# Top-384 sorting network of a 16-expert feed-forward layer: the stages that make runs of 256 go from whole-stage order to two interleaved streams

## What is computed

```python
for i in range(E):                                   # E = 16
    gate_feature = hidden_states * pe[i] @ gate_w + gate_b      # 625 x 768
    gate_weight, gate_idx = jax.lax.top_k(gate_feature, K)      # K = 384
    gate_weight = jax.nn.softmax(gate_weight, axis=-1)
    gathered = jnp.take_along_axis(hidden_states, gate_idx, axis=-1)
    y = y + _moe_mlp(gathered * gate_weight, eg_w[i], eu_w[i], ed_w[i])
```

## Time and profile before

| | us |
|---|---|
| median of 3 runs | 6935.59 (6921.98 to 6955.94) |
| the profiled execution | 6922.95, span 6921.2 |
| DVE busy | 5366.8, 78% of the span |
| PE busy | 5904.7, 85% |
| POOL busy | 3589.6, 52% |
| ACT busy | 2729.2, 39% |
| sort of expert 0 begins | 1287.67 |
| a turn of the loop | 334.0 and 335.0, by turns |

### The profile page before, as it was taken

One profiled execution on the slowest core, in us unless ns is written; L12 is line 12 of the kernel. 1 busy time (PEld: TensorE's weight loads), 2 busy tenths in 40 slices (PEclk: granted clock), 3 DMA queues, 4 the chain that ended last, 5 costly groups with the idle time before them and its releaser, 6 DMA issues. The chain is left out here.

```text
span 6921.2 us, 74102 instructions
## 1 busy us (share of the span) xinstructions
PE 5904.7 (85%) x16985; PEld 3098.9 (45%) x16985; DVE 5366.8 (78%) x6633; ACT 2729.2 (39%) x4297; POOL 3589.6 (52%) x3692
## 2 busy tenths in 40 slices
PE   7979988889797878788888888888888888888988
PEld 5545544445444444343434344434343444444554
DVE  3012003599999999999999999999999999998950
ACT  0000000344544545454545454545454545444531
POOL 2324015356565656565656565656565656555640
PEclk9989999999999999999999999999999999999999
DMA  3356247000000000000000000000000000001001
GB/s 90 102 141 170 104 122 188 26 21 14 14 14 15 14 14 14 14 14 14 14 14 14 14 14 14 14 24 4 28 0 28 14 14 14 14 14 48 15 35 50
DMA packets 118060, 260.81 MB, mean 38 GB/s; under 512 B 39164, under 2 KB 49922, under 8 KB 117682
## 3 DMA queue, kind: packets, MB, share of 16 engines
q1 hardware_dynamic: 70322, 180.18, 7.3%
q0 software_dynamic: 47360, 77.17, 5.0%
HBM read 222.43 MB, written 34.58 MB: 37 GB/s over the span
## 5 line engine op out<-in xcount | busy, mean ns | idle before, releaser
L1183 PE MATMUL mask_ps<-key,neg_ident 125*125 125x480 f32 (+7 forms) x4128 | 1917.1, 584 | 566.5 <-DVE key L1557 563.8
L1285 POOL TENSOR_TENSOR pay<-pay_side,pay 125x240 int32<-125x240 int32 (+6 forms) x1104 | 1045.4, 947 | 1163.7 <-DVE pay L1580 1159.5
L1441 ACT COPY mask_ps<-key 125x960 f32<-125x960 f32 (+7 forms) x1136 | 952.5, 838 | 1462.6 <-DVE pay L1597 762.1
L1183 PEld LDWEIGHTS mask_ps<-key,neg_ident 125*125 125x125 f32 x4128 | 744.7, 194 | 1449.5 <-DVE key L1557 952.1
L1580 DVE COPY_PREDICATED pay<-mask_ps,pay 125x480 f32<-125x480 int32 (+5 forms) x1104 | 1233.8, 1118 | 48.1 <-PE mask_ps L1183 39.4
L1277 POOL TENSOR_TENSOR pay_side<-pay 125x240 int32<-125x240 int32 (+6 forms) x1104 | 1041.7, 944 | 407.5 <-DVE pay L1597 263.7
L1547 DVE TENSOR_TENSOR key<-mask_ps,key 125x480 f32<-125x480 f32 (+5 forms) x1104 | 1088.7, 986 | 60.2 <-PE mask_ps L1183 54.2
L1557 DVE TENSOR_TENSOR key<-mask_ps,key 125x480 f32<-125x480 f32 (+5 forms) x1104 | 1092.1, 989 | 8.3
L1454 ACT COPY pay_side<-pay 125x480 f32<-125x480 f32 (+6 forms) x1104 | 612.4, 555 | 451.8 <-POOL pay L1285 233.2
L1183 PE MATMUL mask_ps<-key_top,neg_ident 125*125 125x480 f32 (+3 forms) x1472 | 591.9, 528 | 229.2 <-DVE key_top L1557 216.6
L1597 DVE COPY_PREDICATED pay<-mask_ps,pay_side 125x480 f32<-125x480 int32 (+6 forms) x1104 | 744.1, 674 | 41.8 <-DVE pay L1580 39.9
(11 more groups left out here) (184 smaller groups left out, 6056.0 us busy)
## 6 DMA issues: line engine op xcount, KB each, us to landing
w_rel<-L_gnn_W SPq DMA_DIRECT2D x16, 2304.0 KB, 23.3
w_exp<-L_ffn_ed_w SPq DMA_DIRECT2D x16, 2304.0 KB, 8.3
messages_dram<-y_out SPq DMA_DIRECT2D x16, 1875.0 KB
w_exp<-L_ffn_eg_w SPq DMA_DIRECT2D x16, 1152.0 KB, 5.4
w_exp<-L_ffn_eu_w SPq DMA_DIRECT2D x16, 1152.0 KB, 7.8
root_w<-L_gnn_root SPq DMA_DIRECT2D x2, 2304.0 KB
w_exp<-L_ffn_sg_w SPq DMA_DIRECT2D x4, 1152.0 KB, 5.9
w_exp<-L_ffn_su_w SPq DMA_DIRECT2D x4, 1152.0 KB, 8.7
```

The source lines that it names most:

```text
L1183: last = pe.matmul(mask, neg_ident[0:TP, 0:TP], operand, start=False, stop=True, skip_group_check=True)
L1285: pool.tensor_tensor(second, shares(pay_was(turn, u), turn, u)[1].bitcast(I32), first, ALU.subtract).then_inc(pays_taken, 1)
L1441: act.copy(seed_of(turn, u), compared(turn, u)[0]).then_inc(seeded, 1)
```

## The change

The ranges of units change, and with them the value of `streams`:

- `streams` now covers stages 28 to 35 as well (`LARGE`). Only `JOIN` is left in whole-stage order.
- Stage 29 is two units of 480 columns where it was one of 960; stage 54 is one of 960 where it was two of 480. A regular turn has 93 units as before: 75 woven, 16 of stages 28 to 35, 2 of `JOIN`. `SORTED` is 37 where it was 39, so exponentials, weights and scaling of the expert before come two units earlier in a turn.
- Stage 28's parts take rows 0 to 31 and 64 to 95 of the 128 places, and 32 to 63 and 96 to 127 (two pieces of 480 columns each), and the first part of stage 30 is one of its three groups instead of two. So stages 28 to 30 can follow each other with one unit between.
- Two points, the first units of stages 28 and 31 (`JOINT`), still need every unit before them. There POOL takes the pays of both units before it adds, and ACT and POOL wait for the second pays of the unit before.

```diff
 UNITS = [(s, part, parts) for s, stage in enumerate(STAGES)
-         for parts in [1 if APART <= s < NS - 1 and comparisons(stage) <= MASK else 2] for part in range(parts)]
+         for parts in [1 if s > JOIN and comparisons(stage) <= MASK else 2] for part in range(parts)]
+JOINT = [APART, STAGES.index(("sort", RUN // 2, RUN // 16))]
@@ class Turn
-        self.needs = [max(u - 1, 0) if u < streams else stages.index(s) for u, s in enumerate(stages)]
+        self.joint = [stages.index(s) for s in JOINT if s in stages]
+        self.needs = [max(u - 1, 0) if u < streams and u not in self.joint else stages.index(s)
+                      for u, s in enumerate(stages)]
@@
-OPENING = Turn(HALVES + WHOLES, len(HALVES), 0)
-REGULAR = Turn(WOVEN + WHOLES, len(WOVEN), 1, OPENING)
+LARGE = [unit for unit in WHOLES if unit[0] < JOIN]
+OPENING = Turn(HALVES + WHOLES, len(HALVES + LARGE), 0)
+REGULAR = Turn(WOVEN + WHOLES, len(WOVEN + LARGE), 1, OPENING)
@@ def part_of
-    cut = (view.shape[dim] + 1) // 2
+    cut = 1 if view.shape[dim] == 3 else (view.shape[dim] + 1) // 2
@@ def part_in_banks
+            if s == APART:
+                quarters = view.rearrange("p n (two x) -> p n two x", two=2)
+                half = quarters.shape[3] // 2
+                return quarters[:, :, :, part * half:part * half + half]
@@ sort of the gpsimd block
-                    if u == turn.streams and u > 1 and turn.shared[u - 2]:
+                    apart = u < turn.streams and u not in turn.joint
+                    if not apart and u > 1 and turn.shared[u - 2] and u <= turn.streams:
                         take_pays(turn, i, u - 2)
-                    ahead = u - 2 if u < turn.streams else u - 1
-                    if ahead >= 0 and turn.shared[ahead]:
+                    ahead = u - 2 if apart else u - 1
+                    if ahead >= 0 and turn.shared[ahead] and u - 1 not in turn.joint:
                         take_pays(turn, i, ahead)
```

## The result

The changed kernel takes 6863.51 us (median of 4 runs, 6852.20 to 6873.89), the kernel before 6932.36 in the runs beside it. The ratio is 0.9902, with a 95% interval of 0.9887 to 0.9917: 69 us or 1.0% faster. The forecast was 6806 us, with 6755 to 6881 as its range. So the direction and the range held, but only a little over half of the 129 us came. The profiled execution took 6858.79 us, its span is 6857.0, which is 64.2 us shorter than the span before.

A forecast was written before the change was run, and what follows sets the result against it. DVE was taken as full before stage 28, and stages 28 to 35 as bound by the order of work. -7.9 us a turn, 126 us over 16 turns, 129 with stage 54, gave 6806 us, range 6755 to 6881.

The forecast's parts named there:

- the order's price: DVE, stages 28 to 35: stream order saves 0.40 us on each of 15 units, -6.0 us a turn.
- the waits of both joints: Stages 28 and 31: new DVE waits for masks and POOL's sums add 3.4 us a turn.
- -7.9 us a turn: Sum for a turn's stages 28 to 35: -6.0 - 2.16 + 0.2 - 4.1 + 0.8 + 3.4.
- The share, -2.2 us: Stages 28 to 35: POOL at 4/8 instead of 3/8 takes 1620 columns a turn of second pays from DVE.
- The waits that go: Stages 28 to 35: DVE's waits for masks and POOL vanish in stream order, -4.1 us a turn.
- the 0.8 us a turn kept for what is late next: Allowance for masks before first pays, POOL's sum and its longer difference ahead of `JOIN`: +0.8 us a turn.
- Two units for one, and one for two, about 0: Stage 29 costs 0.2 us a turn more, stage 54 gives 0.2 back; nothing for work moving two units forward.
- joints at their dear end: Stages 28 and 31: two waits of 3.6 us, with the pays 8.1 us a turn; total 6881 us.
- 1: DVE's own waits are free, the 0.40 us has another cause and stays: 6902 us; chance 0.03.
- 2: POOL's additional work holds up DVE, losing 6.8 us of a turn's 7.9: 6915 us; chance 0.04.
- 3: Waits at stages 28 and 31 and before first pays give everything back: within 20 us of 6935; chance 0.03.
- 4: Joints idle PE, its clock falls and PE becomes the bound in stages 28 to 35: 7016 us; chance 0.05.

The follow-up runs named there:

- the run with 3/8: Changed kernel with POOL's share in stages 28 to 35 at 3/8 as before, instead of 4/8: 6884.9 us.
- The run with the new units alone: Kernel before with only the new list of units (stage 29 two units, stage 54 one), no stream order in stages 28 to 35: 6996.6 us.
- the run with four products moved: Changed kernel with four PE products moved by one unit (7 to 8, 20 to 21, 23 to 24, 30 to 31): 6831.7 us.
- The run with a third joint: Changed kernel with a third point, at stage 33, that needs every unit before it: 6887.9 us.
- closing the first gap: Against ten products moved in the loop alone (6814.8 us): one product moved from 83 to 84, 6817.1 us, or unread products behind unit 84, 6817.6 us.
- closing both: Kernel with unread products behind unit 84, plus three unread products behind unit 28: 6800.3 us.

## Why the prediction was right or wrong

**What held.** The bound of stages 28 to 35 by order, the order's price and the waits of both joints. The four new waits were forecast as 0.95, 0.3, 1.6 and 0.55 us, 3.4 in sum; they are 0.64, 0.42, 1.44 and 0.69, 3.2 in sum. The first is shorter because PE reached the last mask of stage 27 0.06 us behind the minimum, half a microsecond sooner than in the earlier trace rows. The whole of it, -7.9 us a turn, can be checked. Stages 28 to 35 give -120.1 us. The last step of stage 27, which lost its second pays and got the wait in front of the maximum of stage 28, takes 78.4 us in all 16 turns instead of 81.0: -2.6. `JOIN` takes 1.5 more. The sum is -121.2, or 7.6 us a turn. The waits of the earlier trace rows went, apart from the one for the lower clock at unit 87, which stayed in 3 turns of the loop and in that of expert 1.

**Terms of wrong size.** The share, -2.2 us: at the 0.99 ns a column of the run with 3/8, its 1620 columns are 1.6 us. (The run itself moved 1380, as the new units of stage 28 give POOL half either way; against the kernel before, their second pays did go from 600 to 480 columns.) The waits that go were read from three in the earlier trace rows, but the stretch has a fourth of the kind, in front of first pays:

```profile
3846.76 1.24 DVE L1580 COPY_PREDICATED pay<-mask_ps,pay 125x960 f32<-125x960 int32 x1 [0.46 <-PE mask_ps L1183]
```

Over all 16 turns, the waits in the stretch for other engines were 69.4 us, 4.3 a turn and not 4.1. The two errors are small and run opposite ways; the 0.8 us a turn kept for what is late next, of which little came, made good the rest.

**The step that failed.** It is under "Two units for one, and one for two, about 0", with its last sentence, "The 2 units by which exponentials and weights move forward meet the same queues a little earlier; I take nothing for it", and "The products on PE [...] are as before" in the sum. I priced the units by their own instructions and not as the ruler by which `beside` lays out PE's work. The run with the new units alone puts that at 56 us. In the changed kernel the waits of the 13 turns at units 7 to 12, 28 to 35 and 36 to 51 grew by 13.6, 29.0 and 11.2 us, 54 in sum, and the run with four products moved took 39 of them back. That the forecast range of 6755 to 6881 us held the result is luck: its upper edge was worked out for joints at their dear end, and those came as forecast, while what made the time longer was in no term. The diff shows the cut of the units, and `beside` was in the text of the kernel; its rule could have been worked out for both lists before, and would have shown a 480-column unit without a product next to another.

**The rivals.** 1: the own waits cost what the rows said; the steps went from 1.19 and 1.38 us to 1.06 and 1.14 (the latter is what first pays of 960 columns take to the maximum behind, from 3815.38 to 3816.52 above). The rule of the Trainium skill (VectorE: DVE Perf Modes, "The DRAIN you can't avoid"), by which such waits cost nothing, does not hold in the trace after either. 2: POOL doesn't slow DVE's instructions; with its share up, a maximum of 960 columns takes 1.14 us. It costs waits of 0.3 us at the second joint and 0.2 at `JOIN` a turn. 3: most of the gain of the stretch stayed, and the time is outside of 20 us around 6935. 4: the clock was the right thing to fear at the wrong place. With two joints the stretch went from 0.93 to 1.00 in 10 of the 13 turns of the loop and to 0.94 in three. It fell in gaps between products elsewhere, and the waits behind were 0.7 to 3.4 us each. The run with a third joint shows that the fear was not idle: there the stretch was at 0.92 to 0.97 in 11 of the 13 turns.

**What is left open.** In front of stage 28 61.4 us came on top. The last step of stage 27 (-2.6, with its wait) is part of it, so the rest lost 64.0, and 56.4 of that is idleness. The 7.6 left, with some 3 us that the cut of stage 54 should have given, are about 10 us in steps without idleness; where they lie is not shown. Which gap the clock falls in, of several of 2 us, was not found: it changed from turn to turn in one execution, and it moved when another gap was closed.

## What to carry to other kernels

Where background work is laid out by a ruler of the foreground's units, a change of the units moves that work everywhere; work out the layout for both versions, and look at what lies in front of and behind the short units, before the edit is called free. When an engine that serves the critical one has gaps in which its clock can fall, count all the gaps: closing one may only send the fall to the next. Here, closing the first gap gave nothing, and closing both gave 17 us. The waits of a joint between two streams can be priced from the time line, as the latency of what it waits for less the one instruction that still covers it; what it does to the gaps of the engine that serves, and by them to its clock, is a price of its own.

## What the runs showed of the hardware

TensorE's clock does not fall at every gap of the same length. Behind 2.14 and 2.15 us of idleness, the same mask took 2.27 and 1.88 us in two turns of one execution, and a gate product 5.84 and 3.11. Behind 2.96 us, in the run with a third joint, it took 2.67 in one turn and 1.88 in another. Matrix products whose result nobody reads keep the clock up: the granted clock of the stretch was 1.00 in every turn of the loop with them, and 0.94 or 0.97 in 9 of the 13 without. POOL at 62% of the time beside DVE made DVE's instructions no longer: 21.8 us of DVE's busy time were taken over in stages 28 to 35, and the stretch was 17.5 us shorter, the difference being waits.
